# Projections of the second attention: all sums loaded up front by SyncE, queries and keys stored as one run, four store buffers

## The reference, cut to what matters

```python
h = h + y_experts            # two partial sums per token are added to h
x = layernorm(h)
q, k, v = x @ Wq + bq, x @ Wk + bk, x @ Wv + bv      # 16 heads of 16
```

## Time and profile before

| | us |
|---|---|
| median of 3 runs | 2028.17 |
| lowest, highest | 2021.44, 2034.0 |
| the profiled execution | 2023.88 |
| its span | 2022.1 |
| the projections' stage in it, first load to the next stage's first load | 788.65 to 935.88 |

### The profile page before, as it was taken

One profiled execution on the slowest core, in us unless ns is written; L12 is line 12 of the kernel. 1 busy time (PEld: TensorE's weight loads), 2 busy tenths in 40 slices (PEclk: granted clock), 3 DMA queues, 4 the chain that ended last, 5 costly groups with the idle time before them and its releaser, 6 DMA issues. The chain is left out here.

```text
span 2022.1 us, 37307 instructions
## 1 busy us (share of the span) xinstructions
PE 1411.1 (70%) x13394; PEld 1166.5 (58%) x13394; DVE 1053.9 (52%) x3354; ACT 629.3 (31%) x1582; POOL 694.4 (34%) x621
## 2 busy tenths in 40 slices
PE   0537987965789882770876546999843578888884
PEld 0536765745578772550765424777643477777772
DVE  8973444346233331630369954777436845555554
ACT  0001331113134331110477633666321233332221
POOL 6430000006177765300620010201110557777761
PEclk9999997985599996875998867999855689999996
DMA  0000001020299994422126685545003079999995
GB/s 27 1 1 17 1 0 48 21 105 0 81 298 306 297 277 115 110 88 87 43 101 256 255 291 178 168 150 174 1 11 137 0 232 298 304 283 295 288 281 145
DMA packets 144407, 291.80 MB, mean 144 GB/s; under 512 B 28088, under 2 KB 113796, under 8 KB 141716
## 3 DMA queue, kind: packets, MB, share of 16 engines
q1 hardware_dynamic: 104852, 243.75, 34.5%
q0 software_dynamic: 39424, 46.31, 11.3%
HBM read 209.85 MB, written 80.05 MB: 143 GB/s over the span
## 5 line engine op out<-in xcount | busy, mean ns | idle before, releaser
L1190 POOL DMA_INDIRECT moe_sum<-ex_y,moe_idcols x160 | 254.7, 1592 | 125.6 <-ACT ex_y L1270 70.3
L1219 PE MATMUL ex_pg<-ex_xT,ex_w 128*128 128x128 f32 x1280 | 181.7, 286 | 36.0 <-DMA ex_w<-in_m_w 25.0
L1182 POOL DMA_INDIRECT ex_xg<-moe_rows,moe_idcols x160 | 160.5, 1003 | 104.6 <-issue 73.7
L1219 PEld LDWEIGHTS ex_pg<-ex_xT,ex_w 128*128 128x128 f32 x1280 | 158.2, 194 | 57.3 <-issue 28.3
L1748 PE MATMUL bi_ps<-bi_pos,bi_spread 64*32 64x128 f32 x4128 | 139.6, 291 | 66.9 <-ACT bi_spread L1758 49.6
L1219 PE MATMUL ex_pl<-ex_xT,ex_w 128*128 128x128 f32 x1280 | 171.9, 278 | 0.0
L1270 ACT ACTIVATE ex_y<-ex_py,moe_wcols 128x256 f32<-128x256 f32 x160 | 75.8, 474 | 303.2 <-DMA moe_sum<-ex_y,moe_idcols 247.2
L1748 PEld LDWEIGHTS bi_ps<-bi_pos,bi_spread 64*32 64x32 f32 x4128 | 120.0, 115 | 86.5 <-ACT bi_spread L1758 59.7
L1228 PE MATMUL ex_py<-ex_w,ex_mid 128*128 128x256 f32 x640 | 165.2, 381 | 1.0 <-DVE ex_mid L1317 0.6
L1219 PEld LDWEIGHTS ex_pl<-ex_xT,ex_w 128*128 128x128 f32 x1280 | 158.8, 195 | 0.0
L2177 ACT ACTIVATE a_pr<-a_sc,a_nm 128x257 f32<-128x257 f32 x256 | 115.6, 500 | 100.5 <-DVE a_nm L2133 100.4
(11 more groups left out here) (353 smaller groups left out, 2794.8 us busy)
## 6 DMA issues: line engine op xcount, KB each, us to landing
ex_w<-in_m_w SPq DMA_DIRECT2D x160, 771.0 KB, 6.2
a_bt<-attn_bias SPq DMA_DIRECT2D x64, 516.0 KB, 5.8
attn_bias<-bi_T SPq DMA_DIRECT2D x14, 2322.0 KB, 8.4
moe_sum<-rt_zero SPq DMA_DIRECT2D x4, 2304.0 KB, 9.5
pj_yg<-moe_sum POOLq DMA_DIRECT2D x16, 258.0 KB
out_yg<-moe_sum SPq DMA_DIRECT2D x16, 256.0 KB, 3.7
ex_xg<-moe_rows,moe_idcols POOLq DMA_INDIRECT x160
moe_sum<-ex_y,moe_idcols POOLq DMA_INDIRECT x160, 6.0
```

What stands on the lines that cost most here:

```text
L1182: nc.gpsimd.indirect_dma_start(xg[t % R][:], None, m.table, bass.IndirectOffsetOnAxis(idcols[:, t:t + 1], 0)).then_inc(x_in[t % R], 16)
L1190: nc.gpsimd.indirect_dma_start(m.sums[t % 2], bass.IndirectOffsetOnAxis(idcols[:, t:t + 1], 0), y[t % R][:], None, compute_op=ALU.add).the ...
L1219: last = nc.tensor.matmul(banks[q][:, 0, f * P:(f + 1) * P], up(r, c, f0 + f), xT[q][:, c], start=c == 0, stop=c == KC - 1)
```

## The change

- The sums of all 8 images get a buffer each, and SyncE loads them instead of POOL: those of image 0 ahead of the weights, those of images 1 to 7 behind `vb`. No load waits for anything. All of them stand ahead of the first store in SyncE's list.
- Queries and keys lie in one DRAM tensor `qk` of shape (128, 8, 2, 2, 258), so that an image's part is one run of 1032 floats in each partition, and are stored by one DMA. `a.q` and `a.k` are views of it, with other strides than before, for the later stages that read them.
- `qk` and `v` have four buffers instead of two; the waits for `stored` begin at image 4.
- The loops over images are written out on all engines.
- In `attention1_phase` the query column `qt` is loaded by one DMA for each of its two channel blocks instead of one for both, and the waits on it count one more.

```diff
@@ -1325,26 +1325,20 @@
 
     def __init__(self, nc, ph, m):
         self.nc, self.m = nc, m
-        self.yg = [ph.sb(f"yg{q}", [TS, 2, IT, D]) for q in range(2)]
-        self.y_in = [ph.sem(f"y_in{q}") for q in range(2)]
+        self.yg = [ph.sb(f"yg{b}", [TS, 2, IT, D]) for b in range(B)]
+        self.y_in = [ph.sem(f"y_in{b}") for b in range(B)]
...
         self.added = ph.sem("added")
 
-    def loads(self, pool):
-
-
-        for b in range(B):
-            if b >= 2:
-                pool.wait_ge(self.added, b - 1)
-            for z in range(2):
-                self.nc.gpsimd.dma_start(self.yg[b % 2][:, z], self.m.sums[z][b * SP:(b + 1) * SP].rearrange(
-                    "(u p) d -> p u d", p=TS)).then_inc(self.y_in[b % 2], 16)
-
-    def add(self, dve, own, b, q, h):
-
-        rows = h[:, bass.ds(b * IT, IT), :] if not isinstance(b, int) else h[:, b * IT:b * IT + IT, :]
-        dve.wait_ge(self.y_in[q], (b - q) * 16 + 32)
-        own(self.nc.vector.tensor_tensor(rows, rows, self.yg[q][:, 0], ALU.add))
-        self.nc.vector.tensor_tensor(rows, rows, self.yg[q][:, 1], ALU.add).then_inc(self.added, 1)
+    def load(self, sp, b):
+        for z in range(2):
+            sp.dma_start(self.yg[b][:, z], self.m.sums[z][b * SP:(b + 1) * SP].rearrange(
+                "(u p) d -> p u d", p=TS)).then_inc(self.y_in[b], 16)
+
+    def add(self, dve, own, b, h):
+        rows = h[:, b * IT:b * IT + IT, :]
+        dve.wait_ge(self.y_in[b], 32)
+        own(self.nc.vector.tensor_tensor(rows, rows, self.yg[b][:, 0], ALU.add))
+        self.nc.vector.tensor_tensor(rows, rows, self.yg[b][:, 1], ALU.add).then_inc(self.added, 1)
 
...
         self.A = {k[3:]: v for k, v in A.items() if k.startswith("a1_")}
-        self.q, self.k = dram("q", (P, KC, B, SP)), dram("k", (P, KC, B, SP))
+        self.qk = dram("qk", (P, B, 2, KC, SP))
+        self.q, self.k = (self.qk[:, :, n].rearrange("p b c s -> p c b s") for n in range(2))
...
-        qk = [sb(f"qk{q}", [P, 2, KC, SP]) for q in range(2)]
-        v = [sb(f"v{q}", [TS, IT, HEADS, VW]) for q in range(2)]
+        RS = 4
+        qk = [sb(f"qk{n}", [P, 2, KC, SP]) for n in range(RS)]
+        v = [sb(f"v{n}", [TS, IT, HEADS, VW]) for n in range(RS)]
...
-        stored, added_seen = [sem(f"stored{q}") for q in range(2)], sem("added_seen")
+        stored, added_seen = [sem(f"stored{n}") for n in range(RS)], sem("added_seen")
...
         @block.sync
         def _(sp):
+            comb.load(sp, 0)
             sp.dma_start(w[:], a.A["w"]).then_inc(c_in, 16)
             sp.dma_start(cols[:], a.A["bqk"]).then_inc(c_in, 16)
             sp.dma_start(vb[:], a.A["bv"].to_broadcast([TS, D])).then_inc(c_in, 16)
-            with sp.Fori(0, B // 2) as i:
-                for q in range(2):
-                    b = 2 * i + q
-                    sp.wait_ge(comb.added, b + 1)
-                    sp.dma_start(a.h[bass.ds(b, 1)].rearrange("o (u p) d -> p (o u) d", p=TS), h[:, bass.ds(b * IT, IT)]).then_inc(h_out, 16)
-                    sp.wait_ge(q_ready, b + 1)
-                    sp.dma_start(a.q[:, :, bass.ds(b, 1)].rearrange("p c o s -> p c (o s)"), qk[q][:, 0]).then_inc(stored[q], 16)
-                    sp.wait_ge(k_ready, b + 1)
-                    sp.dma_start(a.k[:, :, bass.ds(b, 1)].rearrange("p c o s -> p c (o s)"), qk[q][:, 1]).then_inc(stored[q], 16)
-                    sp.wait_ge(v_ready, b + 1)
-                    sp.dma_start(a.v[bass.ds(b, 1)].rearrange("o (u p) d -> p (o u) d", p=TS),
-                                 v[q][:].rearrange("p u h d -> p u (h d)")).then_inc(stored[q], 16)
-            for q in range(2):
-                sp.wait_ge(stored[q], 48 * (B // 2))
+            for b in range(1, B):
+                comb.load(sp, b)
+            for b in range(B):
+                sp.wait_ge(comb.added, b + 1)
+                sp.dma_start(a.h[b].rearrange("(u p) d -> p u d", p=TS), h[:, b * IT:b * IT + IT]).then_inc(h_out, 16)
+                sp.wait_ge(q_ready, b + 1)
+                sp.wait_ge(k_ready, b + 1)
+                sp.dma_start(a.qk[:, b].rearrange("p m c s -> p (m c s)"),
+                             qk[b % RS][:].rearrange("p m c s -> p (m c s)")).then_inc(stored[b % RS], 16)
+                sp.wait_ge(v_ready, b + 1)
+                sp.dma_start(a.v[b].rearrange("(u p) d -> p u d", p=TS),
+                             v[b % RS][:].rearrange("p u h d -> p u (h d)")).then_inc(stored[b % RS], 16)
+            for n in range(RS):
+                sp.wait_ge(stored[n], 32 * (B // RS))
             sp.wait_ge(h_out, 16 * B)
 
         @block.gpsimd
         def _(pool):
-            for q in range(2):
-                nc.gpsimd.memset(v[q][:], 1.0).then_inc(v_ones, 1)
-            comb.loads(pool)
...
+            for n in range(RS):
+                nc.gpsimd.memset(v[n][:], 1.0).then_inc(v_ones, 1)
...
-            dve.wait_ge(v_ones, 2)
+            dve.wait_ge(v_ones, RS)
...
-                free(dve, stored[q], (b - q) * 24)
+                free(dve, stored[b % RS], b // RS * 32)
...
-            pairs(own.loop(B // 2 - 2, 2 * (norm.OWN + comb.OWN), first=1), step)
+            for b in range(B):
+                step(b, b % 2, b == B - 1)
...
-                free(act, stored[q], (b - q) * 24)
+                free(act, stored[b % RS], b // RS * 32)
...
-            pairs(act.Fori(1, B // 2 - 1), step)
+            for b in range(B):
+                step(b, b % 2, b == B - 1)
...
-            pairs(pe.Fori(1, B // 2 - 1), step)
+            for b in range(B):
+                step(b, b % 2, b == B - 1)
...
-            sp.dma_start(qt[:], a.q[:, :, :, S - 1], allow_slow_non_contiguous=True).then_inc(t_in, 16)
+            for c in range(KC):
+                sp.dma_start(qt[:, c], a.q[:, c, :, S - 1], allow_slow_non_contiguous=True).then_inc(t_in, 16)
...
-            dve.wait_ge(t_in, 16 * (QUADS * B + 3))
+            dve.wait_ge(t_in, 16 * (QUADS * B + KC + 2))
```

More of the change, by code:

```diff
@@ L1561, in _ @@
             own = Own(dve, own_v)
-            dve.wait_ge(v_ones, 2)
+            dve.wait_ge(v_ones, RS)
             def normalised(b, q):
-                comb.add(dve, own, b, q, h)
+                comb.add(dve, own, b, h)
                 dve.wait_ge(comb.added, b + 1)
@@ L1576, in step @@
                     normalised(b + 1, 1 - q)
-                free(dve, stored[q], (b - q) * 24)
+                free(dve, stored[b % RS], b // RS * 32)
                 dve.wait_ge(q_ps, b + 1)
                 for f in range(KC):
-                    last = V.tensor_scalar(qk[q][:, 0, f], pq[:, f, 0:SP], cols[:, 0, f:f + 1], None, ALU.add)
+                    last = V.tensor_scalar(qk[b % RS][:, 0, f], pq[:, f, 0:SP], cols[:, 0, f:f + 1], None, ALU.add)
                 last.then_inc(q_ready, 1)
@@ L1583, in step @@
                 for u in range(IT):
-                    last = V.tensor_tensor(v[q][:, u, :, 0:HD], pv[0:TS, u // 2, (u % 2) * D:(u % 2 + 1) * D].rearrange(
+                    last = V.tensor_tensor(v[b % RS][:, u, :, 0:HD], pv[0:TS, u // 2, (u % 2) * D:(u % 2 + 1) * D].rearrange(
                         "p (h d) -> p h d", d=HD), vb[:].rearrange("p (h d) -> p h d", d=HD), ALU.add)
                 last.then_inc(v_ready, 1)
-            pairs(own.loop(B // 2 - 2, 2 * (norm.OWN + comb.OWN), first=1), step)
+            for b in range(B):
+                step(b, b % 2, b == B - 1)
         @block.scalar
@@ L1596, in step @@
             def step(b, q, last_image):
-                free(act, stored[q], (b - q) * 24)
+                free(act, stored[b % RS], b // RS * 32)
                 act.wait_ge(k_ps, b + 1)
                 for f in range(KC):
-                    last = nc.scalar.activation(qk[q][:, 1, f], pq[:, 2 + f, 0:SP], ACT.Identity, bias=cols[:, 1, f:f + 1])
+                    last = nc.scalar.activation(qk[b % RS][:, 1, f], pq[:, 2 + f, 0:SP], ACT.Identity, bias=cols[:, 1, f:f + 1])
                 last.then_inc(k_ready, 1)
@@ L1991, in _ @@
                 if t == UT:
-                    pool.wait_ge(t_in, 16 * (QUADS * B + 3))
+                    pool.wait_ge(t_in, 16 * (QUADS * B + KC + 2))
                     G.tensor_tensor(h[:, NT1 - 1, :], h[:, NT1 - 1, :], bo[:], ALU.add).then_inc(bo_added, 1)
```

## The result

| | us |
|---|---|
| median after, 4 runs | 2084.06 (2083.35 to 2084.81) |
| median before, 4 runs | 2027.5 (2021.44 to 2034.0) |
| ratio after to before | 1.0285, 95% interval 1.0258 to 1.0312 |
| the profiled execution after, its span | 2083.68, 2081.9 |

A forecast was written before the change was run, and what follows sets the result against it. Two DMA engines carrying SyncE's 86-partition transfers bound the stage: 789.6 + 96.4 (loads) + 106.8 (stores) = 992.8, against 934.0, plus 0.6, is +59.4 us; forecast 2085 us, range 2064 to 2112.

The forecast's parts named there:

- What bounds the kernel now: Second attention's projections: 86-partition stores (`h`, values) all run on the same two DMA engines, 13.35 us an image from image 2.
- The loads on the pair: Sixteen 258 KB sum loads on SyncE's queue all run on those two engines; with weights and bias, 96.4 us at 44.7 KB/us.
- The rivals that the loads spread, wholly or partly: SyncE's sum loads use all 16 engines (2002.5 us, chance 0.07) or four to seven (2017 to 2037, chance 0.05).
- the one that they run at the constants' rate: SyncE's sum loads go at the routing constants' 31 GB/s: 46 us more, 2131 us, chance 0.07.
- The sum: Two engines busy from 789.6 for 96.4 + 106.8 us, to 992.8 instead of 934.0; with 0.6 later, +59.4 us.
- One store for queries and keys: One 516 KB store per image instead of two of 258: priced at nothing, at most 9 us gained in all.
- Order on SyncE: Stores behind all loads cost nothing more, as the two engines stay busy; first `h` store issued near 880.
- Four buffers: Remove ScalarE's 57.9 us of `stored` waits between images 0 and 3; the wait returns once, long, before image 4.
- The unhindered image: An image of the stage not held by stores takes 8.3 us, from the value sums of images 0 and 1.
- POOL's loads not confined: Before, sum loads on POOL's queue were not confined to two engines: slices of 788 to 801 end at 108 to 154 GB/s.
- The second query column load: In the later attention stage, loading the last tokens' query column in two DMAs adds one issue on the path: +0.6 us.

## Why the prediction was right, point by point

**What bounds the kernel now: right, and shown.** Cutting the stores in two, with nothing else changed, takes 2.4% off the kernel before. The rates of one engine (23 GB/s), two (45) and many (200 to 300) are in the runs above.

**The loads on the pair: right.** This was the step that rested on the smallest rows, loads of some 512 bytes. Measured are 5.76 us a load, 258 / 5.76 = 44.8 KB per us, against the 44.7 taken. The rivals that the loads spread, wholly or partly, are dead, and so is the one that they run at the constants' rate: 31 GB/s there is a matter of their short rows or of gaps between small DMAs, which no run tells apart.

**The sum: right, with small errors that cancel.** The stage grew by 59.27 us, against 58.8. The stores take 12.99 us an image instead of 13.35, 8 x 0.36 = 2.9 less. The stretch up to the stores took as much more: the first sums were added at 799.95, 15 us after the first load's issue, where 12.4 were reckoned (801 from 788.65). The slices show where: the rate of two engines is reached at 787.5, 2.5 us after that issue, and the sum lets the pair start 1 us after it.

**One store for queries and keys: priced at nothing, worth 2 us.** 13.27 us an image with two stores and 12.99 with one, 0.28 x 8 = 2.2 us, inside the bound of 9. The two buffers differ as well between these kernels, but the wait that they change lies behind the pair.

**Order on SyncE: right.** The first `h` store was issued at 874.71, 89.7 us after the first load's issue, where 880 - 788.65 = 91.4 was expected, and another order gave the same time.

**Four buffers: right, but for the sign.** The wait came back at image 4, with 41.5 us. It was to stand there once; it stood before each of images 5 to 7 too, for some 9 us, since each needs the slot of an image whose stores leave 13 us apart. The pair is full meanwhile, so it costs nothing.

**The unhindered image: wrong, and without effect.** The 8.3 us were taken where POOL issued loads, which is 0.85 us of them; without these an image takes 7.49 us. Either is shorter than the stores' 13.35, so the sum does not feel it. In the experiment with all transfers cut, where the compute is the bound, the time came out 5.6 us below the expected 1962, and seven images at 0.85 us are 6.0.

**POOL's loads not confined: right, read a little off.** The last eight slices of the earlier trace rows are 102 to 154 GB/s, not 108 to 154. The run with the loads on POOL bears the point out.

**The second query column load: wrong by its 0.6 us.** Both columns hold SyncE for longer than thought, and the 32 small loads behind them for less. Those loads before, then the list after:

```profile
1216.17 14.43 SPq L1938 DMA_DIRECT2D a_btail<-attn_bias  x32
...
1269.30 2.83 SPq L1935 DMA_DIRECT2D a_qt<-attn_qk  x2
1272.17 12.04 SPq L1938 DMA_DIRECT2D a_btail<-attn_bias  x32
1284.25 0.80 SPq L1939 DMA_DIRECT2D a_vtail<-attn_v  x1
1285.10 7.27 SPq L1901 DMA_DIRECT2D a_bt<-attn_bias  x8
1293.65 0.43 DVE L2133 CUSTOM_DVE_ANT_0 a_sc<-a_pss,a_bt 128x257 f32<-128x257 f32 x1 [19.53 <-DMA a_bt<-attn_bias]
```

From the first column's issue to the bias load's it is 15.80 us, against 1231.50 - 1215.57 = 15.93 before; to the end of VectorE's wait it is 1293.65 - 1269.30 = 24.35, against 24.22. SyncE's list is not a sum of issue durations when the queue behind it is full: an issue lasts as long as it takes the queue to have room, and one more of them eats into the next one's wait. The same error would have been large had I priced the 16 loads at their issue duration on an empty queue.

The result thus rests on the steps as they were put; the exact agreement of 2085 with 2084 is partly luck, since the kernel's own runs spread by some 12 us before.

## What to carry to other kernels

A low and even DMA rate was here the rate of few engines: divide it by that of one (22 GB/s here), and look at the partition counts of the transfers under it. A tile of 86 partitions moved by SyncE ran on two engines and one of 43 on a single one. Cutting off the part that divides (80 + 6) costs one more short issue per transfer. Done to all loads and stores, it turned a change that made the stage 59 us longer into one that made it 68 us shorter than before. Before transfers are moved to another queue, ask on how many engines each queue would run that very shape, and sum the bytes per engine over the stage: while one engine was full here, neither order nor buffers mattered. And take the pace of the bare compute from a stretch in which nothing runs beside it that the change removes.

## What the runs showed of the hardware

- The same 258 KB into 86 partitions: two engines at 44 to 46 GB/s when issued by SyncE. From POOL the loads were not so confined; with them on POOL the stage lost its excess.
- Cut in two equal parts, the load did not get faster but slower, 163.08 us for 28 halves against 80.67 for 14 whole ones: the halves did not run beside each other on different engines.
- Issues wait for room. A load's issue of 5.76 us is the time that its predecessors take on the pair, and 28 shorter ones with room take 17.57 / 28 = 0.63 us each.
- POOL's issuing of loads slows VectorE. Three writes of `xn` took 1.91 us beside it and 1.05 us without, and an image 8.34 and 7.49 us, both at a granted clock of 1.00.
- TensorE's granted clock was 1.00 (2.4 GHz) where one image followed the other (7.49 us each) and 0.54, near the level of 1.2 GHz, from 897 to 905 in the changed kernel with cut stores, behind a stretch without matmuls; the image there took 9.63 us.
